# Three experts summed on TensorE, and a reordered front part

## The reference, cut to what matters

```python
# x: 16 samples x 128 tokens x 256 (float32); ctx: the same shape
x = x + tanh(g_xattn) * long_conv(k=ctx, v=ctx, q=layernorm(x))      # 16 heads of 8, causal
# mixture of experts on all T = 16*128 = 2048 tokens
h = rmsnorm(layernorm(x)) * w_norm
probs = softmax(h @ w_router);  w_topk, sel = top_k(probs, 4)         # 32 experts
# each expert takes the first 128 tokens that chose it (CAP = 128) and drops the rest
y_e = (silu(buf_e @ w_gate[e]) * (buf_e @ w_up[e])) @ w_down[e]        # 128x256 -> 176 -> 256
out[token] += y_e[slot] * w_topk                                       # up to 4 experts per token
out += sigmoid(h @ w_shared_gate) * shared_ffn(h)                      # width 704
x = x + tanh(g_ffn) * (layernorm(x) + out)
```

## Time and profile before

| | |
|---|---|
| Median of three runs | 372.09 us (369.93 to 374.17) |
| Profiled execution, its own time | 372.94 us |
| Span in its trace | 371.2 us |
| PE, PEld, VectorE, ACT, POOL busy | 80%, 66%, 58%, 29%, 55% |
| Mean granted TensorE clock | 0.911 |
| Bytes moved | 59.63 MB, 161 GB/s |
| Chain that ended last | PE 43%, DMA 21%, issue 16%, VectorE 10%, POOL 5% |
| A quarter sum read back (256 KB, x24), to landing | 5.5 us median |

### The profile page before, as it was taken

The page is one execution under the profiler, slowest core; times in us unless marked ns, Lnnn a source line. Parts: engine busy times, 40 slices in busy tenths (PEclk is TensorE's granted clock), DMA queues, the critical chain, the costliest instruction groups (busy, mean ns, idle before and its releaser), DMA issues.

```text
span 371.2 us, 4842 instructions
## 1 busy us (share of the span) xinstructions
PE 297.1 (80%) x1482; PEld 244.7 (66%) x1482; DVE 215.3 (58%) x552; ACT 107.2 (29%) x272; POOL 202.5 (55%) x228
## 2 busy tenths in 40 slices
PE   2894688699999889968589798999999999992000
PEld 1893687589988778846567666787777777771000
DVE  3689389988789977896171203222523445447253
ACT  2441026512564004720345103222221333330000
POOL 2881985937689668848705760223333456655300
PEclk9999789789999999998689989999999999997555
DMA  5999999931011111106970004554473699986778
GB/s 174 285 330 292 267 384 376 267 105 66 32 66 64 43 53 53 53 26 170 286 215 6 1 2 128 147 102 89 99 187 86 147 239 228 246 220 172 190 235 296
DMA packets 53385, 59.63 MB, mean 161 GB/s; under 512 B 6731, under 2 KB 48967, under 8 KB 53361
## 3 DMA queue, kind: packets, MB, share of 16 engines
q1 hardware_dynamic: 44576, 49.34, 44.5%
q0 software_dynamic: 7680, 8.95, 12.8%
q10 hardware_dynamic: 1104, 1.05, 0.8%
HBM read 36.83 MB, written 27.21 MB: 173 GB/s over the span
## 4 chain that ended last, share of the span: by engine, by line
PE 43%; DMA 21%; issue 16%; DVE 10%; POOL 5%; ACT 2%; SPq 1%; POOLq 0%; DVEq 0%; ACTq 0%
DMA arena<-in_ctx_dram 9%; PE Y L1106 8%; DMA expert_sum<-arena,ide 7%; PE pg L958 5%; PE pu L958 4%; POOL dispatched L371 4%; PE pd L1125 3%; PE Y L946 3%; PE Y L1125 3%; PE Y L947 3%; PE Y L948 3%; PE pu L987 2%; PE Y L1097 2%; DMA dispatched<-rows,dsu 2%; DVE arena L692 2%
## 5 line engine op out<-in xcount | busy, mean ns | idle before, releaser
L441 POOL DMA_INDIRECT expert_sum<-arena,ide x32 | 51.8, 1618 | 77.3 <-DVE arena L890 67.6
L371 POOL DMA_INDIRECT dispatched<-rows,dsu x64 | 64.1, 1002 | 30.0 <-issue 24.0
L361 POOL TENSOR_TENSOR arena<-arena 128x256 f32<-128x256 f32 x96 | 57.1, 629 | 1.7 <-ACT arena L455 1.3
L946 PE MATMUL Y<-arena 128*128 128x192 f32 x128 | 34.8, 356 | 13.7 <-POOL arena L361 7.1
L877 DVE TENSOR_TENSOR arena<-arena,Y 128x176 f32<-128x176 f32 x32 | 10.8, 338 | 53.8 <-ACT arena L607 51.5
L692 DVE TENSOR_REDUCE arena<-arena 128x128 f32<-128x1024 f32 x32 | 38.8, 1211 | 0.1
L600 ACT ACTIVATE arena<-Y,wn 128x128 f32<-128x128 f32 x64 | 20.0, 364 | 55.3 <-PE Y L1097 55.1
L946 PEld LDWEIGHTS Y<-arena 128*128 128x128 f32 x128 | 23.1, 204 | 17.8 <-issue 10.3
L947 PE MATMUL Y<-arena 128*128 128x192 f32 x128 | 33.4, 345 | 0.0
L948 PE MATMUL Y<-arena 128*128 128x192 f32 x128 | 33.2, 343 | 0.0
L987 PE MATMUL pg<-swd,act 128*128 128x256 f32 (+1 forms) x96 | 28.7, 450 | 2.6 <-DVE act L704 2.1
(11 more groups left out here) (150 smaller groups left out, 595.4 us busy)
## 6 DMA issues: line engine op xcount, KB each, us to landing
expert_sum<-zrow SPq DMA_DIRECT2D x3, 2176.0 KB, 17.0
shared<-expert_sum SPq DMA_DIRECT2D x24, 256.0 KB, 5.5
dispatched<-zrow SPq DMA_DIRECT2D x1, 4624.0 KB, 25.6
arena<-dispatched SPq DMA_DIRECT2D x32, 144.5 KB, 3.2
arena<-in_L_ffn_w_gate_dram SPq DMA_DIRECT2D x22, 176.0 KB
arena<-in_L_ffn_w_up_dram SPq DMA_DIRECT2D x22, 176.0 KB
arena<-in_L_ffn_w_down_dram SPq DMA_DIRECT2D x22, 176.0 KB
arena<-taps SPq DMA_DIRECT2D x4, 512.0 KB, 5.9
```

The lines of the kernel that those rows point to most:

```text
L361: ins = pool.tensor_tensor(o[:, :, blk], i0, i1, ALU.mult)
L371: pool.indirect_dma_start(buf, bass.IndirectOffsetOnAxis(ap=dsu[:, t % 2, j:j + 1], axis=0), rows[:, t % 2, j // K, :], None, bounds_check ...
L441: pool.indirect_dma_start(accs[a], bass.IndirectOffsetOnAxis(ap=ide[:, e % NO:e % NO + 1], axis=0), ye[:, e % NO, :], None, compute_op=ALU ...
L946: pe.matmul(yv[:, 0], TT[:, h, P:L], kvv[:, 0], start=True, stop=True)
```

## The change

- **Last three experts (OWN = 3).** Experts 29 to 31 are no longer scatter-added. VectorE builds a one-hot matrix for each, 128 rows by 2048 tokens, in four instructions of 512 columns (`onehot_part`, during e = 24 to 29) from an iota that POOL makes. ACT rounds their results to float32r (`y_high`) and VectorE takes the rest (`y_low`). PE multiplies: for each of 16 samples, three experts and two parts, one 256-column matmul into all eight PSUM banks (`own`, 96 in all). VectorE adds bank `i` to its pair of samples.
- **Accumulators.** Number 0 is no longer zeroed; SP writes the base rows `x_sb` into it (four DMAs of 512 KB) when the last unit is done, placed at e = 12. Experts 0 to 14 go to 1 and 2, 15 to 23 to all three, 24 to 28 to 0 and 1. VectorE now forms sum 1 + sum 2, then adds sum 0, then PE's part: 24 additions for the sums and PSUM together become 8 + 8 + 8. Sum 2 is read in four parts. Stores are issued by ACT's queue.
- **Weights.** Expert 16 + e is loaded at expert e.
- **Units.** Unit 28 moves into the expert loop (twelve instead of eleven). The `down` products start on the other bank, and wait for the last of the six parts only before it is used.
- **Front part.** `more_ctx(2)` goes ahead of the last load of x and the zeroing of `buf`; `products(1, 0..3)` ahead of `query_pow(2)`; `out_tr(t, 0)` ahead of `k_tr`/`q_tr`; for the last group `xn_high` ahead of `lg_copy`, `exps` and a silu, and `token_pow` one send earlier.

```diff
-CLOSE, TAIL = 24, 2
+OPEN, CLOSE, OWN = 15, 24, 3
+ADDED = E - OWN
-UNITS_EXPERT = range(29, 40)
+UNITS_EXPERT = range(28, 40)
 def down_out(b):
-    return (pg, pu)[b % 2][:, 0:L]
+    return (pu, pg)[b % 2][:, 0:L]
+def own_out(i):
+    return (pg, pu, Y[:, 2], Y[:, 0], Y[:, 1], pm, pd, Y[:, 3])[i][:, 0:2 * L]
 def sum_of(e):
-    if e < CLOSE:
-        return e % 3
-    return e % 2 if e < E - TAIL else 0
+    if e < OPEN:
+        return 1 + e % 2
+    return e % 3 if e < CLOSE else e % 2
 # SP
+            more_ctx(2)
             load_x(sp, 3)
             sp.wait_ge(s["z_ready"], 1)
             sp.dma_start(buf..., zrow...)
-            more_ctx(2)
-            for a in accs:
+            sp.dma_start(accs[0][B * S:, :], zrow[:, 0:L]).then_inc(s["acc_init"], 16)
+            for a in accs[1:]:
-            PACE = [e + 3 * e // 4 for e in range(E - NW)]
+            PACE = range(E - NW)
             for e in range(E):
+                if e == len(UNITS_EXPERT):
+                    sp.wait_ge(s["down_used"], GB * G)
+                    for i in range(G):
+                        sp.dma_start(accs[0][i * GB * S:...], x_sb[:, GB * i:GB * (i + 1), :]).then_inc(s["base_in"], 16)
 # POOL
+            for p in range(4):
+                products(1, p)
             query_pow(2)
-            for p in range(4):
-                products(1, p)
-            for i in range(1, 4):
+            for i in range(1, 3):
                 send(G - 2, i)
             token_pow(G - 1)
+            pool.iota(iota_t, pattern=[[1, OHN]], ...)
-            for e in range(E):
+            for e in range(ADDED):
+                if e == OPEN:
+                    pool.wait_ge(s["base_in"], 16 * G)
 # ACT, last token group
             xn_evac(t, 1)
+            for c in range(2):
+                xn_high(t, c)
             lg_copy(t)
             exps(t)
             silu(LATE + 4)
-            for c in range(2):
-                xn_high(t, c)
+            def y_high(e):
+                act_e.wait_ge(s["e_yout"], e + 1)
+                act_e.activation(y_split[HI][:, e - ADDED], ye[:, e % NO, :], ACT.Copy).then_inc(s["y_high"], 1)
 # VectorE
+            def onehot_part(i, k):
...
+                ins = dve.tensor_scalar(onehot[:, i, k * OHN:(k + 1) * OHN], iota_t, xe[:, (ADDED + i) % NX, ROW - 1:ROW],
+                                        -1.0 * k * OHN, ALU.subtract, ALU.is_equal)
+            def y_low(e):
+                dve.wait_ge(s["y_high"], e - ADDED + 1)
+                dve.tensor_tensor(y_split[LO][:, e - ADDED], ye[:, e % NO, :], f32(y_split[HI][:, e - ADDED]), ALU.subtract)
 # PE
+            def own(i, b, e):
+                for part in (HI, LO):
+                    ins = pe.matmul(own_out(i)[:, b * L:(b + 1) * L], onehot[:, e, (2 * i + b) * S:(2 * i + b + 1) * S],
+                                    y_split[part][:, e], start=(e == 0 and part == HI), stop=(e == OWN - 1 and part == LO))
...
+            for i in range(2 * G):
+                for b in range(2):
+                    for e in range(OWN):
...
+                            ins = own(i, b, e)
+                ins.then_inc(s["own_done"], 1)
```

More of the change, by code:

```diff
@@ L215, in flamingo_block @@
         add_sem = [sem(f"added{i}") for i in range(3)]
[L216 removed]
+        FINE = (2, 2, 1)
+        fin_sem = [[sem(f"sum{a}_in{i}") for i in range(FINE[a] * G)] for a in range(3)]
         def sum_of(e):
[L219 to L221 removed]
+            if e < OPEN:
+                return 1 + e % 2
+            return e % 3 if e < CLOSE else e % 2
         def adds_before(e):
@@ L226, in all_added @@
         def all_added(a):
-            return 16 * sum(sum_of(e) == a for e in range(E))
+            return 16 * sum(sum_of(e) == a for e in range(ADDED))
         def load_x(eng, g):
@@ L314, in load_sum @@
                 sp.wait_ge(add_sem[a], all_added(a))
-                for i in range(2 * G):
-                    sp.dma_start(sums[a][:, i], accs[a][i * 2 * P:(i + 1) * 2 * P, :].rearrange("(b p) l -> p b l", p=P)
+                n = FINE[a] * G
+                rows_ = B * S // n
+                for i in range(n):
+                    sp.dma_start(sums[a][:, i * B // n:(i + 1) * B // n], accs[a][i * rows_:(i + 1) * rows_, :].rearrange("(b p) l -> p b l", p=P)
                                  ).then_inc(fin_sem[a][i], 16)
-            sp.wait_ge(s["down_used"], GB * G)
             load_sum(2)
@@ L424, in _ @@
                         send(t, 0)
-            for i in range(1, 4):
+            for i in range(1, 3):
                 send(G - 2, i)
             token_pow(G - 1)
-            for i in range(4, 8):
+            for i in range(3, 8):
                 send(G - 2, i)
@@ L903, in _, with x_pair, add_own @@
                     use(UNITS_EXPERT[e])
-            def add_sum(a, i):
-                dve.wait_ge(fin_sem[a][i], 16)
-                xs = x_sb[:, 2 * i:2 * i + 2, :]
-                return dve.tensor_tensor(xs, xs, sums[a][:, i], ALU.add)
-            for a in (2, 1):
-                for i in range(2 * G):
-                    ins = add_sum(a, i)
-                link(ins)
-            for i in range(2 * G):
-                add_sum(0, i).then_inc(s["fin_add"], 1)
+                for k in range(4 * OWN):
+                    if ONEHOT_AT + k // 2 == e:
+                        onehot_part(k // 4, k % 4)
+                if e > ADDED:
+                    y_low(e - 1)
+            y_low(E - 1)
+            def x_pair(i):
+                return x_sb[:, 2 * i:2 * i + 2, :]
+            dve.wait_ge(s["base_in"], 16 * G)
+            for i in range(2 * G):
+                dve.wait_ge(fin_sem[2][i // 2], 16)
+                dve.wait_ge(fin_sem[1][i], 16)
+                k = mark(dve.tensor_tensor(x_pair(i), sums[1][:, 2 * i:2 * i + 2], sums[2][:, 2 * i:2 * i + 2], ALU.add))
+            after(k)
+            two = {}
+            def add_own(i):
+                dve.wait_ge(s["own_done"], i + 1)
+                after(two[i])
+                dve.tensor_tensor(x_pair(i), x_pair(i), own_out(i).rearrange("p (b l) -> p b l", b=2), ALU.add).then_inc(s["fin_add"], 1)
+            for i in range(2 * G):
+                dve.wait_ge(fin_sem[0][i], 16)
+                two[i] = mark(dve.tensor_tensor(x_pair(i), x_pair(i), sums[0][:, 2 * i:2 * i + 2], ALU.add))
+                if i:
+                    add_own(i - 1)
+            add_own(2 * G - 1)
         @block.tensor
@@ L1059, in _ @@
                         conv(g + 1, 0)
+                    if p == 0:
+                        out_tr(t, 0)
                     if p < 4 and g + 1 < G:
```

70 lines of the change are left out of this document (55 added, 15 removed).

## The result

The changed kernel takes 362.07 us (median of 4 runs, 360.52 to 362.89) against 372.23 for the kernel before (369.93 to 374.17, 4 runs); the ratio is 0.972 with an interval of 0.966 to 0.979. Measured again with more runs it took 360.13 (8 runs, ratio 0.965, 0.960 to 0.970). Medians here are of all runs, while ratios and their intervals leave out single runs that lasted over 1.5% longer than the fastest of the same kernel, so a ratio is not exactly the quotient of two medians. The forecast was 358.6: right in direction and in most of its causes, a little too good in size. The profiled execution took 361.41 us with a span of 359.6, so the time outside the span is 1.8, as before, and spans can be set against each other: 371.2 to 359.6.

What follows compares the result with a forecast made beforehand. No single engine was taken to bound the run; each stage has its own late thing. The sum was 372.94 - 7.1 - 4.5 + 2.8 + 2.0 - 7.5 = 358.6 us, with 351 to 367 for 8 in 10.

Steps and rivals of the forecast that it cites:

- Context and products earlier: Front part: context ahead of the zeroing and products ahead of `query_pow(2)` start the first addition to x at 40.7, -7.1 us.
- Rounding earlier: Token group 3: rounding and subtracting before the slots are ready gains 5.5, less 1.0 for a slower cast, -4.5 us.
- PE's units early enough: Before the first expert: PE's units end up to 6.7 us earlier, enough for an expert start 4.5 earlier.
- One more unit among the experts: Expert stage: PE has no gap there, so unit 28 adds its 2.79 us, +2.8.
- Base rows and weights at every expert: Expert stage from e = 12: these bytes delay later experts' rows, so PE waits 0 to 5 us, +2.0 taken.
- One-hots: Late experts: VectorE's twelve instructions, 1.4 us per two, leave it just full with slack before PE, 0; bounds 0 and 1.5.
- The rival by which they would slow the scatter-adds: Late experts: one-hots stretch the issue of the adds of experts 24, 26 and 28 by 2.2 each, 365.2 us; chance 0.08.
- The trap of the Trainium skill: Scatter-adds beside one-hots: GpSimd can't write its descriptors while VectorE is in a two-port mode; cited for the 0.08 rival.
- The end: After the experts: expert 28's add lands last at 340.8 to 344.5, VectorE's additions end at 358.5, the span at 363.7, -7.5.
- gains cancel: Whole kernel: front gains nothing, dispatch 2.5, stall 5, end 3, giving 372.2 us; chance 0.05.

Runs made afterwards that it cites:

- unit 28 back: The changed kernel with unit 28 in front of the experts again (29 to 39 among them): 357.34 us, ratio 0.959 to the kernel before.
- front only: The kernel before with only the five reorderings of the front part: 362.3 us, ratio 0.970; again with more runs 362.6 us, 0.974.
- context late: The changed kernel with the load of the second half of context behind the zeroing loads again: 361.65 us, ratio 0.969 to the kernel before.

## Why the prediction was right, step by step

**Context and products earlier, -7.1: -5.95 at the addition, -5.3 at token group 3.** Right mechanism for PE's and POOL's waits, with a small error of size: VectorE's copy blocked beside a subtraction for 1.4 us. The `mult` behind the reduce took about 0.2 less than the 1.4 costed. The reading of the chain was half right. The chain names the transfer, and it did end last; but with the new orders of PE and POOL the first addition doesn't wait for it even when it is late: the load's place was worth 0.2 at this milestone. What I had put first, the transfer, did next to nothing for this addition; that `out_tr` ahead, which I called "part of it", is what frees the addition from the load is argued from PE's order and was not tried alone.

**Rounding earlier, -4.5: -4.49 at the first send** (-9.77 less the -5.28 by which group 3's sums came earlier). Against the variant with that half of the step undone it is 3.2. The cast charged with 1.0 took 1.47 longer; what arrived at the slots was 0.8 against the kernel before (7.23 for 6.42 us from the cast's start) and about 0.5 against the variants, so the charge was a little too high for the path. The page of the Trainium skill, SBUF — State Buffer, "Who interferes with whom" (a cast beside GpSimd's reads is blocked for the whole instruction) is borne out for the cast: 1.43 to 2.71 in six traces, 0.18 to 0.24 otherwise. By that page I had worked out 3.0 for the step with both subtractions blocking. Both did block, but the one cast came 0.9 us into them and part of its delay fell into a wait; the measured 3.2 to 4.5 lies above the 3.0.

**PE's units early enough: true, but at the price of a cold start, +1.5.** I had worked out that up to 6.7 us were there and called it enough. It was more than enough: PE finished 2.72 us too early, and its clock fell. I had that very effect in a row, a product at 4.71 after 2.06 of idling, and used it for the end part only. This term was missing from the sum; "unit 28 back" shows it, with the gap closed and the products at 1.35.

**One more unit among the experts, +2.8: +2.9** between the first expert and the fourteenth. Its place in front was the gap of 2.72: back there it costs 0.2 (23.8 us from first send to first transpose, for 23.6).

**Base rows and weights at every expert, +2.0: +3.3**, inside its bounds of 0 to 5. Mechanism right, shown by taking either of its two causes away.

**One-hots, 0: +0.55** from expert 20 to the last down product (bound 1.5). The two of an expert took 0.87 us, not 1.4. The rival by which they would slow the scatter-adds is refuted: the adds issued from 318 us on, among the one-hots, took 1.55 to 1.64 each. Nor do the additions beside it explain the 3.77 of the earlier trace rows: in the same place of the old end part one add took 3.50 us in "front only" and 1.69 in its repetition. The trap of the Trainium skill (SBUF — State Buffer, "SBUF: two separate sides") did not show.

**The end, -7.5: -10.07.** The add of expert 28 was last and landed early, as worked out, and PE's products cost 0.12 each (0.115 forecast). Reads and pair sums closed 12.8 us after the last down product against 11.7; but the 16 additions came every 0.60 us, not 0.69 (9.8 for 11.0), and 2.7 us followed VectorE where I had taken 5.2 from the old end. There, the eight stores' issues took 6.53 us and closed only with the last; now they are spread along the additions (8.18 us). That this spread is what shortened the tail was not tried by itself.

Sum of the errors: +1.2 at the first addition, +0.6 between it and token group 3's send, +1.5 cold start, +1.3 stall, +0.1 unit, +0.6 one-hots, -2.6 end, total +2.7. The span came out at 359.6 against 356.9, by 2.7. An end part better by 2.6 covered half of the 5.3 lost in the front part and the expert stage; that much of the near hit is luck. One rival was added up wrongly: the terms of "gains cancel" as written give 375.2, not 372.2; both lie within 1% of the kernel before.

## What to carry to other kernels

When a step is moved so that its consumer's data come earlier, work out also how early the consumer itself is done: a gap of 2.7 us ahead of the experts cost TensorE's clock on top of the gap, and one unit of filler in it cost 0.2 us. A burst that fits the average rate of a stage still stalls it; the same bytes one group at a time, where the rate has room, cost nothing. A wait's releaser on the chain need not be what must be moved: look at what stands behind that wait in the same engine's order without needing it. And an instruction that takes 1.5 us longer need not delay its consumer by 1.5: measure from its start to the place that counts, and first see how far that place moves between two traces of the same code.

## What the runs showed of the hardware

- TensorE after idling: ahead of the first expert, where a gap of 2.67 to 2.75 us is followed by another of 0.81, the next products took 2.55 us instead of 1.35 in all six traces that have it; with 1.50 ahead of the 0.81 (context late) they took 1.79 and the next ones 2.43, and with the 0.81 alone (four traces) 1.35. Among the experts a gap of 2.12 and one of 2.70 were followed by products at 1.35, and one of 1.99 by products at 2.55. So the length of the gap alone doesn't decide, and a forecast should carry both cases.
- A VectorE cast or copy beside GpSimd's two-input subtraction: 1.43 to 2.71 us instead of 0.18, and 1.95 instead of 0.56, while the subtraction (two instructions) itself took 2.50, the same as without a cast beside it. The cast ended 0.04 to 0.05 after the second instruction, the copy 0.03 after the first of its two. With POOL idle the same copy took 0.16.
- In the end part, in the ten traces with the new end and the new pace of weights, the add of expert 27, with the read of a sum ended or within 2.2 us of its end, landed in 3.67 to 3.98 us, and that of expert 25, issued about a microsecond after the 2 MB read of a sum began, in 7.42 to 8.04.
- TensorE products from float32r with 256 columns: 0.12 us each at full clock, half of the 0.23 for 512.
- Two-operand additions of VectorE of 128 x 512 show 0.68 us each and start every 0.60 us: the spacing, not the duration, is what a chain of them costs.
